# Adaptive-norm FFN with Strassen products on one core: two loads of SyncE's queue put in front of the first fetch of conditioning weights

## The chip, the cores and the metric

One core of a Trainium2 chip. The metric is the device time of one execution in microseconds (us); lower is better. The kernel before has 432.35 us as the median of 3 runs.

## The reference, cut to what matters

```python
W = L0_cond_weights[itok_B_0_15]                  # (64, 64, 64) picked out of 16 matrices
y = einsum('bct,bcd->bdt', x, W)                  # x: (64, 64, 1024), fp32
top1 = argmax(y_flat @ gate_w.T + expert_bias)    # 4 experts
base = einsum('bth,oh->bto', y, W_up)             # W_up: 1024 x 1024
delta = (y_flat @ lora_A[top1].T) @ lora_B[top1].T  # rank 8
out = x + base + delta
```

## The kernel before, in words

The 64 batch entries are taken in pairs (128 rows: two entries of 64 channels), and two pairs make a block, so there are 16 blocks of 256 rows. The product with W_up (1024 x 1024) is done for each block by a Strassen-like scheme of seven products of half size, named a11, a12, a22, s1, s2, s4 and s3. Each operand is split in a high and a low part, and a product is three matmuls per slice of 128. For that the rows of W_up must be transposed on TensorE (`turn_weights`, L632; L662), some of them after a sum or difference of quarters (`subtract`, L264: kinds 1 to 4, each for a row group c from 0 to 3), and every transposed group of 128x512 is then rounded by ScalarE (`split_turned`, L477; L493) and its low part made by VectorE (L893). There are 31 such groups in a written-out order, `TURNS` (L217), and PSUM banks are passed from one to another: a group waits until VectorE has finished the one that had its bank.

W_up arrives as eight pieces of 512 KB (`load_w_up`, L313), w_raw[0] to w_raw[7]; here they are called W0 to W7. The x of a pair is 512 KB too, x0 to x3 for the first two blocks. The first two blocks do not wait for the whole conditioning table. For each of their four pairs SyncE loads two indices into registers and fetches just the two 16 KB matrices that are needed (`load_first_cond`, L303; L309) into the tile y_small, which GpSimd has zeroed. TensorE needs both fetches and the x of the pair for `make_first_y` (L623, matmuls at L627), and ScalarE copies the result out (`move_first_y`, L439; L441). In later blocks `make_y` uses the whole table.

All these loads are issued on SyncE's queue in this order: W6, W7, W3, lora_B, W4, fetch 0 (two DMAs of 16 KB), x0, W2, W0, W5, W1, fetch 1, x1, x2, half of the table, x3, the other half, fetch 2, fetch 3. ScalarE issues the index, router and bias loads at the start.

TensorE's order in the start-up is written out at L735 to L815: warm-up transposes between the first groups (L738), then s4 of W4, two groups of lora_B, two warm-up transposes (L754), `make_first_y(0, 0)` (L756), s2 of W3, a11 of W2 (L758), `make_first_y(0, 1)`, s1 of W6, a12 of W2, a11 of W0 and so on; the first products (L679) follow. Block 1 onwards is a steady loop. In the start-up GpSimd does most of the `subtract` steps (L384 to L397), VectorE three of them (L1024, L1036, L1059) and the first `add_s1` (L1046, printed as L286), whose two inputs lie in SBUF.

Of the kernel before, what the change touches and what calls it, by code (L numbers as in the profile page):

```python
# [5 lines left out]
def adaln_ffn_kernel(  # L6
# [34 lines left out]

    B, C, T = x.shape
    S, _, D = cond_weights.shape
    O, _ = w_up.shape
    E, R, _ = lora_a.shape
# [24 lines left out]
    with ctx:  # L70
# [116 lines left out]
        def in_blocks(eng, period):  # L187
            with eng.Fori(0, BLOCKS // 2 - 1) as group:
                for n in range(2):
                    period(group * 2 + (n + 1), (n + 1) % 2, False)  # L190
            period(BLOCKS - 1, (BLOCKS - 1) % 2, True)

        def is_last(q):
            return isinstance(q, int) and q == BLOCKS - 1
# [4 lines left out]
        def x_part(par, t, half):  # L199
            return x_sb[:, 2 * par + t, half * BANK:(half + 1) * BANK]  # L200
# [9 lines left out]
        def first_cond(t):  # L210
            return y_small[:, t * P:(t + 1) * P]
# [10 lines left out]
                 ("a22", 3, p1)]  # L222
        GROUPS = [(op, c) for op, c, _ in TURNS]
        BANK_OF = [bank for _, _, bank in TURNS]
        FREED_BY = []
        for g in range(len(GROUPS)):
            same = [f for f in range(g) if BANK_OF[f] == BANK_OF[g]]
            FREED_BY.append(same[-1] + 1 if same else 0)
        LAST_OF = {op: 1 + max(g for g, (o, _) in enumerate(GROUPS) if o == op) for op, _ in GROUPS}
        AT = {name: g for g, name in enumerate(GROUPS)}  # L230

# [69 lines left out]
        @block.sync  # L301
        def _(sp):
            def load_first_cond(t):  # L303
                sp.wait_ge(index_loaded, 16)
                sp.wait_ge(first_zero, 1)
                for b in range(2):
                    rows = slice(b * C, (b + 1) * C)
                    index = sp.value_load(index_sb[0:1, 2 * t + b:2 * t + b + 1], min_val=0, max_val=S - 1)
                    sp.dma_start(first_cond(t)[rows, b * D:(b + 1) * D],  # L309
                                 cond_weights[bass.ds(index, 1), :, :].rearrange("s c d -> (s c) d"))\  # L310
                       .then_inc(first_loaded[t], 16)

            def load_w_up(c):  # L313
                sp.dma_start(w_raw[:, c, :], w_up[c * P:(c + 1) * P, :]).then_inc(w_up_loaded[c], 16)

            load_w_up(6)
            load_w_up(7)
            load_w_up(3)
            sp.dma_start(lora_b_sb[:, :, :, :], lora_b.rearrange("e (p j) r -> p e j r", p=P)).then_inc(lora_b_loaded, 16)
            load_w_up(4)  # L320
            load_first_cond(0)
            sp.dma_start(x_sb[:, 0, :], x_pairs[0]).then_inc(x_loaded[0], 16)
            load_w_up(2)
            load_w_up(0)
            load_w_up(5)
            load_w_up(1)
            load_first_cond(1)
            sp.dma_start(x_sb[:, 1, :], x_pairs[1]).then_inc(x_loaded[1], 16)
            sp.dma_start(x_sb[:, 2, :], x_pairs[2]).then_inc(x_loaded[2], 16)
            sp.dma_start(cond_sb[0:C, :, :], cond_rows).then_inc(cond_loaded[0], 16)  # L330
            sp.dma_start(x_sb[:, 3, :], x_pairs[3]).then_inc(x_loaded[3], 16)
            sp.dma_start(cond_sb[C:2 * C, :, :], cond_rows).then_inc(cond_loaded[1], 16)
            load_first_cond(2)
            load_first_cond(3)

            def store(q, par, t, half):
                sp.dma_start(out_pairs[2 * q + t, :, half * BANK:(half + 1) * BANK], x_part(par, t, half))\
                    .then_inc(stored[t], 16)

            def store_quarter(q, par, n):  # L340
                cols = slice(n * QUARTER, (n + 1) * QUARTER)
                sp.dma_start(out_pairs[2 * q + 1, :, cols], x_sb[:, 2 * par + 1, cols]).then_inc(stored[1], 16)

            def period(q, par, closing):
                sp.wait_ge(c11_out, q + 1)
                store(q, par, 0, 0)
                sp.wait_ge(c12_out, q + 1)
                store(q, par, 0, 1)
                if is_last(q):
                    sp.wait_ge(c21_out, q + 1)  # L350
                    store_quarter(q, par, 0)
                    sp.wait_ge(c22_out, q + 1)
                    store(q, par, 1, 1)
                    sp.wait_ge(last_out, 1)
                    store_quarter(q, par, 1)
                else:
                    sp.wait_ge(c21_out, q + 1)
                    store(q, par, 1, 0)
                    sp.wait_ge(c22_out, q + 1)
                    store(q, par, 1, 1)  # L360

            period(0, 0, False)
            in_blocks(sp, period)
            for t in range(2):
                sp.wait_ge(stored[t], 32 * BLOCKS + 16 * t)
# [802 lines left out]
```

## Time and profile before

| | |
|---|---|
| median of 3 runs | 432.35 us (431.86 to 432.89) |
| the profiled execution | 432.26 us, of which the span is 430.4 us |
| TensorE busy | 424.5 us (99% of the span) |
| VectorE busy | 358.3 us (83%) |
| ScalarE busy | 190.9 us (44%) |
| GpSimd busy | 117.4 us (27%) |
| granted TensorE clock | 1.000, mean |
| DMA | 38.85 MB, mean 90 GB/s |

PE is TensorE, ACT ScalarE, DVE VectorE, POOL GpSimd and SP SyncE; a q behind the name is the engine's queue. A row of the timeline gives the start in us from the start of the span, the duration, engine and line, then tile written and tiles read, and how many instructions were merged. Successive instructions of an engine overlap by some tenths of a microsecond. "us to landing" counts from an issue's start to the last of its data.

### The profile page before, as it was taken

What the parts mean: (1) busy time and instruction counts of PE and PEld (TensorE: products, weight loads), DVE (VectorE), ACT (ScalarE), POOL (GpSimd) and SP (SyncE); (2) the same over time, 40 slices, a digit from 0 to 9 for tenths busy, and PEclk for the clock granted to TensorE, in tenths of its full rate; (3) what the DMA queues carried; (4) which work ended last, traced back from release to release, by engine and by line L of the source; (5) the groups of instructions that cost most, each with busy time, mean ns of one, the idle gap of its engine ahead of it and who ended that gap; (6) DMA issues with size and microseconds to landing.
All of it is one profiled execution on the core that took longest, in us unless ns stands there. A gap on an engine that the chain in (4) does not pass through costs nothing.

```text
span 430.4 us, 8609 instructions
## 1 busy us (share of the span) xinstructions
PE 424.5 (99%) x2937; PEld 396.8 (92%) x2938; DVE 358.3 (83%) x648; ACT 190.9 (44%) x301; POOL 117.4 (27%) x92
## 2 busy tenths in 40 slices
PE   7999999999999999999999999999999999999997
PEld 7989999999999999999999999999999999999996
DVE  2998489797979979797997979799797989979773
ACT  3973463363625336262543626254263625426220
POOL 4971140503205050220505023050502305050230
DMA  7930140502214041230403123050312304031202
GB/s 266 353 55 3 50 149 24 170 18 86 96 44 151 24 130 42 86 107 34 161 24 123 47 79 116 24 171 24 122 49 64 131 24 171 24 122 49 80 19 97
DMA packets 18582, 38.85 MB, mean 90 GB/s; under 512 B 5094, under 2 KB 5350, under 8 KB 18570
## 3 DMA queue, kind: packets, MB, share of 16 engines
q1 hardware_dynamic: 14336, 23.86, 15.7%
q10 hardware_dynamic: 4234, 14.83, 11.4%
q8 instruction: 7, 0.11, 0.1%
q14 instruction: 5, 0.04, 0.0%
HBM read 21.91 MB, written 16.78 MB: 90 GB/s over the span
## 4 chain that ended last, share of the span: by engine, by line
PE 95%; ACT 3%; DVE 1%; issue 0%; POOL 0%; DVEq 0%; POOLq 0%; ACTq 0%
PE bank_x L679 23%; PE bank_y L679 23%; PE bank_c L679 20%; PE y_ps L619 11%; PE bank_b L679 10%; PE bank_x L738 1%; PE bank_y L685 1%; PE bank_x L685 1%; PE bank_c L685 1%; PE bank_b L685 1%; ACT w_s L493 1%; PE y_ps L627 1%; ACT w_a L493 1%; PE bank_y L716 1%; DVE w_s L893 0%; PE bank_c L694 0%
## 5 line engine op out<-in xcount | busy, mean ns | idle before, releaser
L286 POOL TENSOR_TENSOR s_sum<-a 128x512 f32<-128x512 f32 x15 | 19.5, 1301 | 283.4 <-DVE a L867 264.9
L432 ACT ACTIVATE x_hl<-x_sb 64x1024 fp32r<-64x1024 f32 x56 | 59.1, 1055 | 34.5 <-DMA out_dram<-x_sb 29.9
L862 DVE TENSOR_TENSOR x_hl<-x_sb,x_hl 64x1024 fp32r<-64x1024 f32 x56 | 68.3, 1220 | 1.7
L436 ACT ACTIVATE y_small<-y_ps 128x512 f32<-128x512 f32 x56 | 33.5, 597 | 57.7 <-PE y_ps L619 57.7
L619 PE MATMUL y_ps<-cond_hl,x_hl 128*128 x448 | 58.1, 273 | 0.0
L619 PEld LDWEIGHTS y_ps<-cond_hl,x_hl 128*128 128x128 f32 x448 | 54.7, 191 | 1.5 <-issue 0.2
L679 PE MATMUL bank_x<-w_a,hl_a 128*128 128x256 f32 (+1 forms) x408 | 54.1, 288 | 0.0
L679 PEld LDWEIGHTS bank_x<-w_a,hl_a 128*128 128x128 f32 x408 | 52.7, 188 | 0.4
L867 DVE TENSOR_TENSOR a<-y_ps,y_small 128x512 f32<-128x512 f32 x56 | 38.5, 687 | 16.7 <-ACT y_small L436 16.7
L679 PE MATMUL bank_y<-w_s,hl_s 128*128 128x292 f32 (+1 forms) x384 | 51.6, 290 | 0.0
L679 PE MATMUL bank_x<-w_s,hl_s 128*128 128x292 f32 (+1 forms) x384 | 51.5, 290 | 0.0
L679 PE MATMUL bank_y<-w_a,hl_a 128*128 128x292 f32 (+1 forms) x384 | 51.1, 289 | 0.0
L679 PEld LDWEIGHTS bank_y<-w_s,hl_s 128*128 128x128 f32 x384 | 49.8, 188 | 0.8 <-issue 0.2
L679 PEld LDWEIGHTS bank_x<-w_s,hl_s 128*128 128x128 f32 x384 | 49.8, 188 | 0.6
L679 PEld LDWEIGHTS bank_y<-w_a,hl_a 128*128 128x128 f32 x384 | 49.7, 188 | 0.2
L679 PE MATMUL bank_c<-w_s,hl_s 128*128 128x512 f32 x192 | 48.2, 399 | 0.0
L679 PE MATMUL bank_b<-w_s,hl_s 128*128 128x512 f32 x192 | 48.1, 399 | 0.0
L446 ACT ACTIVATE hl_a<-a 128x512 fp32r<-128x512 f32 x48 | 30.5, 636 | 36.1 <-DVE a L867 33.6
L679 PEld LDWEIGHTS bank_c<-w_s,hl_s 128*128 128x128 f32 x192 | 34.9, 188 | 7.3
L679 PEld LDWEIGHTS bank_b<-w_s,hl_s 128*128 128x128 f32 x192 | 35.2, 190 | 6.7
L679 PE MATMUL bank_c<-w_a,hl_a 128*128 128x512 f32 x168 | 41.2, 394 | 0.0
L872 DVE TENSOR_TENSOR hl_s<-s_sum,hl_s 128x512 fp32r<-128x512 f32 x32 | 37.2, 1170 | 3.5 <-ACT hl_s L446 2.0
(119 smaller groups left out, 566.8 us busy)
## 6 DMA issues: line engine op xcount, KB each, us to landing
out_dram<-x_sb SPq DMA_DIRECT2D x63, 256.0 KB, 2.0
x_sb<-in_x_dram ACTq DMA_DIRECT2D x28, 512.0 KB, 3.7
w_raw<-in_L_ffn_W_up_dram SPq DMA_DIRECT2D x8, 512.0 KB, 7.4
x_sb<-in_x_dram SPq DMA_DIRECT2D x4, 512.0 KB, 8.4
cond_sb<-in_L_cond_weights_dram SPq DMA_DIRECT2D x2, 256.0 KB, 9.6
out_dram<-x_sb SPq DMA_DIRECT2D x2, 128.0 KB, 1.9
router_sb<-in_L_ffn_lora_A_dram ACTq DMA_DIRECT2D x1, 128.0 KB
lora_b_sb<-in_L_ffn_lora_B_dram SPq DMA_DIRECT2D x1, 128.0 KB, 7.8
```

The source lines that it names most:

```text
L286: eng.tensor_tensor(s1_sum[:, :], a21[:, :], a22[:, :], ALU.add).then_inc(s1_added, 1)
L432: act.activation(x_hl[rows, t, b, :], x_sb[rows, 2 * par + t, :], ACT.Copy).then_inc(x_high, 1)
L436: act.activation(y_small[:, :].rearrange("q (g d) -> q g d", d=D), halves_of(y_ps)[:, :, 1, :], ACT.Copy).then_inc(y_small_out, 1)
L446: act.activation(hl[op][:, 0, :, :], src[:, :].rearrange("q (k n) -> q k n", n=P), ACT.Copy)\
L493: act.activation(turn_target(op, c, 0), bank.rearrange("q (k n) -> q k n", n=P), ACT.Copy)\
L619: mm = pe.matmul(y_ps[:, k % KH // 2, at:at + P], x_hl[:, t, b, k * P:(k + 1) * P], cond_hl[:, index[b], :, :], start=True, stop=True)
L627: mm = pe.matmul(FIRST_Y[2 * t + h][:, k * P:(k + 1) * P], x_sb[:, t, (h * KH + k) * P:(h * KH + k + 1) * P], first_cond(t), start=True, s ...
L679: mm = pe.matmul(dst, hl[op][:, a, k, :], w[:, b, k, cols], start=(fresh and k == 0 and a + b == 0), stop=(k == KH - 1 and a == 1), skip_g ...
L685: return pe.matmul(dst, z_t[t][:, :], src, start=False, stop=True, skip_group_check=True)
L862: dve.tensor_tensor(x_hl[other, t, b, :], x_sb[rows, 2 * par + t, :], x_hl[rows, t, b, :].bitcast(fp32), ALU.subtract).then_inc(x_low, 1)
L867: dve.tensor_tensor(dst[:, :].rearrange("q (g d) -> q g d", d=D), halves_of(y_ps)[:, :, 0, :], y_small[:, :].rearrange("q (g d) -> q g d", ...
L872: dve.tensor_tensor(hl[op][:, 1, :, :], src[:, :].rearrange("q (k n) -> q k n", n=P), hl[op][:, 0, :, :].bitcast(fp32), ALU.subtract).then ...
```

## The change

Of the two loads behind fetch 0, x0 and W2, both are now issued in front of it. Everything else keeps its place.

```diff
@@ -318,9 +318,9 @@
             load_w_up(3)
             sp.dma_start(lora_b_sb[:, :, :, :], lora_b.rearrange("e (p j) r -> p e j r", p=P)).then_inc(lora_b_loaded, 16)
             load_w_up(4)
-            load_first_cond(0)
             sp.dma_start(x_sb[:, 0, :], x_pairs[0]).then_inc(x_loaded[0], 16)
             load_w_up(2)
+            load_first_cond(0)
             load_w_up(0)
             load_w_up(5)
             load_w_up(1)
```

## Rows read from the trace of the kernel before

**Rows 1.** The page: shares of the chain that ended last, by engine.

```profile
PE 95%; ACT 3%; DVE 1%; issue 0%; POOL 0%; DVEq 0%; POOLq 0%; ACTq 0%
```

**Rows 2.** The chain that ended last, 0 to 55 us: start, us, what.

```profile
12.01 0.60 ACT w_s L493
...
22.38 0.50 ACT a L441
...
28.38 0.18 DVE partial L967
...
31.55 0.61 DVE w_raw L282
...
32.92 3.03 PE bank_x L679 x24
```

**Rows 3.** Timeline of SyncE's queue, 2.6 to 9.4 us.

```profile
2.65 0.69 SPq L314 DMA_DIRECT2D w_raw<-in_L_ffn_W_up_dram  x1
4.42 1.85 SPq L309 DMA_DIRECT2D y_small<-in_L_cond_weights_dram  x2
6.32 0.59 SPq L322 DMA_DIRECT2D x_sb<-in_x_dram  x1
6.95 2.38 SPq L314 DMA_DIRECT2D w_raw<-in_L_ffn_W_up_dram  x4
```

**Rows 4.** DMA issues: W4, fetch 0's second, x0, W2, fetch 3's last.

```profile
w_raw<-in_L_ffn_W_up_dram SPq DMA_DIRECT2D x1, 512.0 KB, 8.6
...
y_small<-in_L_cond_weights_dram SPq DMA_DIRECT2D x1, 16.0 KB, 5.8
...
x_sb<-in_x_dram SPq DMA_DIRECT2D x1, 512.0 KB, 6.3
...
w_raw<-in_L_ffn_W_up_dram SPq DMA_DIRECT2D x1, 512.0 KB, 7.0
...
y_small<-in_L_cond_weights_dram SPq DMA_DIRECT2D x1, 16.0 KB, 2.2
```

**Rows 5.** Windows: length, busy PE, PEld, DVE, ACT, POOL, granted clock, DMA share, GB/s.

```profile
12.00:13.00 1.00, 1.00 (x11) 1.00 (x10) 1.00 (x3) 0.99 (x2) 1.00 (x2) 1.00 1.06 430
...
17.00:32.00 15.00, 14.83 (x117) 13.78 (x115) 15.00 (x25) 12.33 (x24) 12.68 (x9) 1.00 0.58 124
```

**Rows 6.** Timeline of TensorE, 1.5 to 17 us.

```profile
1.53 3.46 PE L738 MATMUL bank_x<-ident 128*128 128x128 f32 x15 [1.53 <-POOL ident L371]
...
8.61 0.68 PE L640 MATMUL bank_c<-ident,router_sb 36*128 36x36 f32 x8 [1.20 <-DVE w_s L893]
...
12.90 1.06 PE L627 MATMUL y_ps<-y_small,x_sb 128*128 128x128 f32 x8
...
14.66 1.06 PE L627 MATMUL bank_y<-y_small,x_sb 128*128 128x128 f32 x8
...
15.99 1.04 PE L662 MATMUL y_ps<-ident,w_raw 128*128 128x128 f32 x8
```

**Rows 7.** Timeline of ScalarE, around 15.8 us.

```profile
15.84 0.62 ACT L441 ACTIVATE a<-bank_y 128x512 f32<-128x512 f32 x1
```

**Rows 8.** Timeline of VectorE, 17 to 25.5 us.

```profile
17.04 0.68 DVE L893 TENSOR_TENSOR w_s<-bank_c,w_s 128x512 fp32r<-128x512 f32 x1
17.63 0.72 DVE L270 TENSOR_TENSOR w_raw<-w_raw 128x512 f32<-128x512 f32 x1
...
21.86 0.68 DVE L872 TENSOR_TENSOR hl_a<-a,hl_a 128x512 fp32r<-128x512 f32 x1
...
23.66 1.80 DVE L286 TENSOR_TENSOR s_sum<-a 128x512 f32<-128x512 f32 x1
```

**Rows 9.** Timeline of GpSimd, 17.7 to 26.7 us.

```profile
17.76 1.75 POOL L278 TENSOR_TENSOR w_raw<-w_raw 128x512 f32<-128x512 f32 x1
...
23.63 1.28 POOL L282 TENSOR_TENSOR w_raw<-w_raw 128x512 f32<-128x512 f32 x1
...
24.87 1.75 POOL L282 TENSOR_TENSOR w_raw<-w_raw 128x512 f32<-128x512 f32 x1
```

## The prediction, made before the changed kernel ran

> **What bounds the kernel now.** I read the page first, for what the end hangs on. TensorE makes 95% of the chain that ended last [rows 1]; from 32.92 us on the chain is TensorE's products one behind another [rows 2]. So whatever shift the start-up has at 32.9 us arrives whole at the end, and the question is what sets that moment. The chain says it: ScalarE from 12.01 to 22.88 us without a gap, then TensorE, VectorE from 28.38 until its subtract ends at 32.16, then TensorE again [rows 2]. From 17 to 32 us VectorE is busy for all of the 15 us and TensorE for 14.83 [rows 5]. Three engines are nearly full there, and the chain changes between them.
>
> Next I read the loads, since the change touches only their order. SyncE finishes issuing W4 at 3.34 us, spends 1.08 us on the index registers, issues the two fetches from 4.42 to 6.27, x0 from 6.32, W2 from 6.95 [rows 3]. With the landing times of [rows 4], W4 lands at 2.65 + 8.6 = 11.25; the second fetch, issued in the last half of its row at about 5.8, at 5.8 + 5.8 = 11.6; x0 at 6.32 + 6.3 = 12.6; W2 at 6.95 + 7.0 = 13.95. They land in the order of issue, about 1.3 us apart for 512 KB, although a fetch of 16 KB would be small work; and the engines move 430 GB/s at 12 to 13 us, with a DMA share above 1 [rows 5]. I read this as one backlog served in order: SyncE issues some 6 us ahead of what lands.
>
> Last, the consumer. TensorE's first product with x0 has its first matmul at 12.90 [rows 6], right behind x0's landing at 12.6; the fetch was there 1.3 us before it. So x0 has no slack and the fetch has 1.3.
>
> **The change, part by part.**
>
> *SyncE.* x0 and W2 are issued from about 3.4 to 4.5 us (0.59 and some 0.5 us). Index loads and the fetches (1.08 + 1.85) follow and end near 7.4. W0 is issued within 0.1 us of where it was; W5, W1, fetch 1 and the rest don't move. No wait is added; the index wait is merely later. Cost on the issuing side: nothing.
>
> *The landings.* x0 and W2 have no longer the two fetches in front of them; these took what W4 to x0 (1.35 us) has over an ordinary 1.3, about 0.1. So x0 lands near 12.5 and W2 near 13.85. Gain: none on TensorE, since its warm-up transposes run until about 12.8 anyway. The fetch now lands behind W2 as it landed behind W4, 11.6 - 11.25 = 0.35 later: 13.85 + 0.3 = 14.1, at most 13.95 + 0.35 = 14.3. From the other side, if a fetch took its 5.8 us from issue whatever stands before it, its second half, now issued near 7.0, lands at 12.8. I take 14.1, because the rows show spacing by bytes in order, not a fixed delay: the last fetch of 16 KB, issued when the backlog was gone, took 2.2 us and not 5.8 [rows 4].
>
> The Trainium skill, DMA: Bandwidth & Descriptors, section "Anatomy of one DMA", puts a transfer at about 2.0 us plus its bytes at 436 GB/s (for GpSimd's path). By it a 16 KB fetch issued at 7.0 would land near 9.1, as an estimate from that page, before x0, and the change would cost nothing. The 2.2 us of the late fetch agrees with the page, the 5.8 us in the loaded stretch does not.
>
> *TensorE.* A first matmul follows a landing it waited for by some 0.15 us (I take this between 0 and the 0.3 by which 12.90 lies behind x0), so it starts at 14.26 instead of 12.90: 1.36 us later. All that stands behind it in TensorE's order moves too: s2 of W3, a11 of W2, the second half of y0 (matmuls from 14.66, end 15.72 [rows 6]), s1 of W6, the pair of groups at 15.99. W2 is not late for any of them.
>
> *ScalarE.* It copied the second half of y0 at 15.84 [rows 7], 0.12 us after TensorE ended it. Now that ends at 15.72 + 1.36 = 17.08 and the copy starts at 17.12: 1.28 us later. ScalarE is contiguous from there to 22.88 [rows 2], so it regains nothing by itself.
>
> *VectorE.* The low part at 17.04 [rows 8] becomes one at about 18.28 (TensorE, then ScalarE in front of it): 1.24 later. Behind it stands its own subtract, L270, at 17.63, now at 18.87. Here the order of two engines matters. The rows show that VectorE and GpSimd stand in each other's way when both read two SBUF operands: GpSimd's 1.28 us step took 1.75 beside L270 [rows 8, 9]; VectorE's L286, started at 23.66 just behind GpSimd's of 23.63, took 1.80 instead of 0.7 and ended 0.55 after GpSimd's end at 24.91; and GpSimd's next, from 24.87, ended 1.16 after VectorE's 25.46. Whoever is first finishes first. GpSimd's step of 17.76 (L278, W0) needs a11 of W0 transposed, which ends at 15.99 + 1.04 = 17.03, now 18.39. So it starts at 18.43, in front of VectorE's L270, and ends at 19.72; L270 ends at 19.72 + 0.55 = 20.27 instead of 18.35. Shift on VectorE: 1.92.
>
> From there each walks at its own pace. GpSimd waits for L270, then has three steps of 1.25 (W1, W0, W1): 20.31, 21.56, 22.79 to 24.08. VectorE's a11 operand (at 21.86 [rows 8]) comes at 21.86 + 1.92 = 23.78, is held to 24.63 (0.17 more) and holds GpSimd's fourth step to 24.63 + 1.16 = 25.79. VectorE reaches L286 at 23.66 + 1.92 + 0.17 = 25.75, and GpSimd its last L282 step at 25.75. It is a tie. If VectorE is first, L286 ends at 25.75 + 0.72 = 26.47, against 25.46 before: shift 1.0, since the wait of 1.1 us that it had is gone. If GpSimd is first, L286 ends at 25.75 + 1.28 + 0.55 = 27.6: shift 2.1.
>
> VectorE is contiguous from L286 to 32 us [rows 5]; at 28.38 it takes TensorE's first product, which, 1.4 to 1.6 us later, is still done before VectorE comes to it at 29.4. So the chain carries VectorE's shift: 1.0 in the first case, 2.1 in the second. TensorE, which waits for VectorE once more before 32.9, arrives there with 1.0 to 1.1, or 2.1.
>
> **The sum.** 1.36 on TensorE, 1.24 on VectorE, + 0.68 (L270 held) + 0.17 (operand held) - 1.1 (L286 not held) = 1.0, and 0.1 for TensorE's own lateness: **+1.1 us**. The profiled execution took 432.26 us, span 430.4; the sum gives 433.35. It lies 0.1 under the median of the runs, so on the median I forecast 432.35 + 1.1 = 433.45, put at **433.5**.
>
> **A rule on the two engines.** The Trainium skill, SBUF — State Buffer, says that VectorE and GpSimd share one pair of SBUF ports under an exclusive lock: the one that starts first keeps it for its whole instruction and the other is blocked, for a VectorE instruction with two SBUF inputs too. The 1.80 us of L286 agrees. Without this rule every shift would be the plain 1.24 to 1.36, and the sum +1.3.
>
> **The rivals.**
>
> *GpSimd wins the tie at L286*: all as above, +2.1, so 434.45. For it: before, GpSimd was ahead by 0.03 us there; against: two starts worked out to a tenth decide nothing. From 0.05 us on it decides whole.
>
> *The small fetch isn't behind W2*: it lands at 12.8 or earlier, TensorE starts within 0.1 us of before, and the time is 432.35 to 432.5. This is the case in which the change doesn't do what its order suggests. For it: the fetch is small, 32 KB in all. Against: it landed behind W4 before, and x0 behind it [rows 4]. The absorbed shift (waits that I think full turn out slack) comes to the same side: 432.4 to 433.0.
>
> *Faster*: one mechanism, the 1.1 us that VectorE's L286 spends behind GpSimd [rows 8]. If the fetch lands in time or nearly so, and the small shifts (x0 and W2 earlier by 0.1) put VectorE's L286 in front of GpSimd's step, at a TensorE delay under 0.5 us, the net is -0.2 to -1.1: 431.3 to 432.1. It decides from 0.03 us of order at 23.6; against it stand the landings.
>
> *The clock*: TensorE idles 1.3 us in front of y0. Before, it idled 1.20 us in front of 8.61 [rows 6], the granted clock is 1.00 in these windows [rows 5] and 1.000 as the mean of the span, and the transposes afterwards ran at 0.11 us each. If it fell to the lower of its two levels (1.2 of 2.4 GHz): the first 15 transposes took 3.46 us, 0.23 each, twice that pace; a stretch like it costs 3.46 / 2 = 1.7 more, in all 435.2. The Trainium skill, TensorE: Matmul & The Clock Gate, Part 1, has idleness close the gate again; the 1.20 us gap did not.
>
> **How the numbers follow.** Chances: the forecast 0.42; GpSimd first 0.27; fetch in time or shift absorbed 0.20; faster 0.06; clock 0.03; 0.02 for what I don't see. The range reaches from the fetch in time to GpSimd first with the landing at its late bound (+0.2 and something for noise): 432.2 to 434.8. A measurement of this kernel can tell about 0.2% (0.86 us) from no change. The forecast lies close above that at +1.1, so I give a fifth of it to "same", and with the rivals: slower 0.65, same 0.28, faster 0.07.
>
> **What would show it.** On SyncE's queue, x0 at 3.4 and the fetches at about 5.5 to 7.3. The fetch landing 7 us after its issue, x0 some 9 us after its own. TensorE idle about 1.3 us before its first L627 matmul, at 14.2 and released by that load; ScalarE's copy at 15.84 now near 17.1. VectorE's L270 at 1.4 us instead of 0.72, and L286 at 0.7 (forecast) or 1.8 (first rival). The first product of the second row of the chain (32.92) at 33.9 to 35. If TensorE's first L627 starts before 13.1, the backlog reading is wrong; if it starts at 14.2 and the end is not later by a microsecond, the chain through ScalarE and VectorE was not as full as I read it.

## The result, and the profile after

The changed kernel takes 435.36 us (435.12 to 435.42, 4 runs) against 432.36 us: 3.0 us more, ratio 1.0061 with a 95% interval of 1.0035 to 1.0087 (ratios here and below are the recorded ones; the two medians alone give 1.0069). A second set of 10 runs gave 435.38 us, ratio 1.0059 (1.0043 to 1.0076). It is slower, as forecast, but by 3.0 us and not 1.1, outside the range (432.2 to 434.8). The profiled execution took 435.42 us, its span 433.6.

The chain that ended last, 0 to 60 us of the kernel after (start, us, what):

```profile
6.77 7.84 DMA y_small<-in_L_cond_weights_dram
14.61 0.14 issue
14.75 1.13 PE y_ps L627 x8
...
19.50 1.43 DVE w_raw L270
...
24.52 0.86 DVE hl_a L872
...
26.63 3.30 PE bank_x L679 x24
...
34.53 0.61 DVE w_raw L282
...
35.91 3.04 PE bank_x L679 x24
```

Before, no DMA stood in this stretch of the chain, and ScalarE's groups filled it up to 22.88 us [rows 2]. Now it starts with the second half of the small fetch, which takes 7.84 us to land, and then TensorE, a short piece of ScalarE, and VectorE from 18.80 to 26.59 us. TensorE's first product (26.63) waits for VectorE's last low part there, and from 30.76 us on the chain is VectorE's again. L286 and the steps next to it run beside that product and are not in the chain as the profile draws it; VectorE is nevertheless busy without a gap from 19.50 us on, so its delays add up in its own timeline, below. The product that was at 32.92 in [rows 2] is at 35.91: +2.99, the whole difference.

SyncE's queue of the kernel after, from 2.6 to 9.8 us (SPq is SyncE's queue):

```profile
2.65 0.63 SPq L314 DMA_DIRECT2D w_raw<-in_L_ffn_W_up_dram  x1
3.33 0.50 SPq L321 DMA_DIRECT2D x_sb<-in_x_dram  x1
3.87 0.45 SPq L314 DMA_DIRECT2D w_raw<-in_L_ffn_W_up_dram  x1
5.39 1.95 SPq L309 DMA_DIRECT2D y_small<-in_L_cond_weights_dram  x2
7.38 2.43 SPq L314 DMA_DIRECT2D w_raw<-in_L_ffn_W_up_dram  x3
```

DMA issues of the kernel after, one by one: W4, x0, W2, the fetch's second half (KB, us to landing):

```profile
w_raw<-in_L_ffn_W_up_dram SPq DMA_DIRECT2D x1, 512.0 KB, 8.9
...
x_sb<-in_x_dram SPq DMA_DIRECT2D x1, 512.0 KB, 9.5
...
w_raw<-in_L_ffn_W_up_dram SPq DMA_DIRECT2D x1, 512.0 KB, 10.4
...
y_small<-in_L_cond_weights_dram SPq DMA_DIRECT2D x1, 16.0 KB, 7.8
```

W4 lands at 11.55, x0 at 12.8, W2 at 14.3, the fetch at 14.6, in the order of issue. x0 is issued 3.0 us earlier than before and lands 0.2 us later. TensorE, the timeline of the kernel after:

```profile
14.75 1.13 PE L627 MATMUL y_ps<-y_small,x_sb 128*128 128x128 f32 x8 [1.36 <-DMA y_small<-in_L_cond_weights_dram]
```

It starts 1.85 us behind its 12.90 of [rows 6], and TensorE was idle for 1.36 us in front of it. Then ScalarE, VectorE and GpSimd, the timelines of the kernel after, with the rows that answer to [rows 7 to 9]:

```profile
17.68 0.60 ACT L441 ACTIVATE a<-bank_y 128x512 f32<-128x512 f32 x1 [0.19 <-PE bank_y L627]
```

```profile
18.80 0.69 DVE L893 TENSOR_TENSOR w_s<-bank_c,w_s 128x512 fp32r<-128x512 f32 x1 [0.48 <-ACT w_s L493]
19.50 1.43 DVE L270 TENSOR_TENSOR w_raw<-w_raw 128x512 f32<-128x512 f32 x1
...
24.44 0.94 DVE L872 TENSOR_TENSOR hl_a<-a,hl_a 128x512 fp32r<-128x512 f32 x1
...
26.50 1.81 DVE L286 TENSOR_TENSOR s_sum<-a 128x512 f32<-128x512 f32 x1
...
29.43 0.81 DVE L872 TENSOR_TENSOR hl_s<-s_sum,hl_s 128x512 fp32r<-128x512 f32 x1
```

```profile
19.10 1.28 POOL L278 TENSOR_TENSOR w_raw<-w_raw 128x512 f32<-128x512 f32 x1 [0.86 <-PE y_ps L662]
...
24.78 1.73 POOL L282 TENSOR_TENSOR w_raw<-w_raw 128x512 f32<-128x512 f32 x1
...
26.48 1.28 POOL L282 TENSOR_TENSOR w_raw<-w_raw 128x512 f32<-128x512 f32 x1
```

In GpSimd's rows L278 is `subtract` of kind 2 and L282 of kind 4. Read VectorE's starts against [rows 8]: +1.76 at 18.80, +1.87 at L270. L270 is 0.71 longer, because GpSimd's L278 had begun at 19.10 and ran until 20.38; before, L270 was first by 0.13 us. L872 is 0.26 longer (GpSimd's third step of kind 2 was running). L286 is as long as before, 1.81, and starts 2.84 late: GpSimd's last L282 was 0.02 us in front of it. L872 at 29.43 is 0.13 longer. That makes 1.87 + 0.71 + 0.26 + 0.13 = 2.97.

TensorE's first product started here in the kernel before:

```profile
24.21 3.27 PE L679 MATMUL bank_x<-w_a,hl_a 128*128 128x292 f32 x24
```

Now it starts at 26.63 and ends at 29.93, 2.4 us late, because VectorE's low part in front of it ends at 26.59. So TensorE itself was 2.4 us late by then, and VectorE 3.0.

### The profile page after: what moved, and what is told of

Its sections match the earlier page's. It is cut to its first block, busy times and chain, and to the rows that moved or that the text cites. A ratio compares the mean times of both kernels' runs of the same rounds, so it can differ in the third digit from the quotient of the medians.

```text
span 433.6 us, 8609 instructions
## 1 busy us (share of the span) xinstructions
PE 426.1 (98%) x2937; PEld 396.8 (91%) x2938; DVE 360.4 (83%) x648; ACT 191.3 (44%) x301; POOL 116.6 (27%) x92
## 4 chain that ended last, share of the span: by engine, by line
PE 93%; DVE 3%; DMA 2%; SPq 1%; issue 0%; ACT 0%; DVEq 0%
PE bank_x L679 23%; PE bank_y L679 23%; PE bank_c L679 19%; PE y_ps L619 11%; PE bank_b L679 10%; DMA y_small<-in_L_cond_weights_dram 2%; PE y_ps L627 1%; DVE w_s L893 1%; PE bank_x L685 1%; PE bank_y L685 1%; PE bank_c L685 1%; PE bank_b L685 1%; DVE w_a L893 1%; PE bank_y L716 1%; SPq L314 1%; PE bank_c L694 0%
## 5 line engine op out<-in xcount | busy, mean ns | idle before, releaser
L286 POOL TENSOR_TENSOR s_sum<-a 128x512 f32<-128x512 f32 x15 | 19.5, 1301 | 283.5 <-DVE a L867 265.0
L872 DVE TENSOR_TENSOR hl_s<-s_sum,hl_s 128x512 fp32r<-128x512 f32 x32 | 38.1, 1197 | 2.7 <-ACT hl_s L446 1.0
```

Of the source, the lines that this page charges most:

```text
L286: eng.tensor_tensor(s1_sum[:, :], a21[:, :], a22[:, :], ALU.add).then_inc(s1_added, 1)
L872: dve.tensor_tensor(hl[op][:, 1, :, :], src[:, :].rearrange("q (k n) -> q k n", n=P), hl[op][:, 0, :, :].bitcast(fp32), ALU.subtract).then ...
```

## The experiments

Twelve kernels ran. The first two are the pair again, unchanged. Where nothing else is said, the lines are an edit of the changed kernel. Ratios are against the kernel before, run beside each set.

**e1_before.** No edit.

> The kernel before, unchanged, to see how much the load stream moves from one profiled execution to the next. In the two traces at hand W4 lands at 11.27 us before and 11.59 after the change, and the loads behind it are 0.34 to 0.5 us later too, although nothing in front of W4 was moved. Theory A (that lateness varies from execution to execution): W4 lands anywhere from 11.2 to 11.6 here, W2 2.7 us behind it, and the time is 431.9 to 432.9. Theory B (the two earlier issues slow the stream themselves): W4 lands at 11.25 to 11.3 here.

Measured: 432.47 us, ratio 1.000 (0.9983 to 1.0017), W4 8.7 us from issue to landing against 8.6 in [rows 4].

**e2_after.** No edit.

> The kernel after, unchanged, as the pair of the run above. Both theories: fetch 0 lands 0.3 us behind W2, TensorE's first product with x0 starts 0.15 us behind that, and the time is near 435.4. Theory A: W4 lands between 11.2 and 11.6; where it is early, the first product starts at 14.4 instead of 14.75. Theory B: W4 lands at 11.55 to 11.65 again.

Measured: 435.38 us; W4 8.9 us again, first product at 14.86. Theory A falls: here and below, the four profiles with the order of before have W4 at 8.6, 8.7, 8.7 and 8.6 us from its issue (always at 2.65 to 2.70), the nine that issue something else right behind W4 have 8.8 to 9.3. The loads from W4 on are late with the new order, W4 itself included.

**e3_x0_only.** Shown against the kernel before.

```diff
-            load_first_cond(0)
             sp.dma_start(x_sb[:, 0, :], x_pairs[0]).then_inc(x_loaded[0], 16)
+            load_first_cond(0)
             load_w_up(2)
```

> Only x0 in front of fetch 0; W2 stays behind it. The theory of a backlog served in order: the fetch lands 0.3 us behind x0, near 12.9 to 13.2, and TensorE's first product with x0 starts 0.2 to 0.5 us later than before. If shifts are carried plainly, the time is 432.6 to 432.9. If the port order between VectorE and GpSimd adds to them: VectorE's L270, which was 0.13 us ahead of GpSimd's L278, falls behind it, takes 1.2 to 1.9 us instead of 0.72, and the time is 433.4 to 434.0. The rival that a small fetch overtakes 512 KB loads: no difference to before.

Measured: 434.35 us, ratio 1.0035 (1.0017 to 1.0053), single runs from 432.96 to 435.15. Its profiled execution is one of 434.55 us. TensorE, VectorE and GpSimd in it:

```profile
13.76 1.02 PE L627 MATMUL y_ps<-y_small,x_sb 128*128 128x128 f32 x7
...
18.51 1.73 DVE L270 TENSOR_TENSOR w_raw<-w_raw 128x512 f32<-128x512 f32 x1
...
18.41 1.28 POOL L278 TENSOR_TENSOR w_raw<-w_raw 128x512 f32<-128x512 f32 x1
```

The product is 0.86 late, more than I expected. In this execution two things end together in front of it: the fetch lands at 13.65 (issued at 6.35, 7.3 us to landing), and W4, 9.3 us from its issue, landed at 11.9 and TensorE worked from then on without a gap until 13.70. So this run alone doesn't show that the fetch held the product. L270 costs another 1.01, since GpSimd was ahead by 0.10 us. 0.9 us of lateness became 2.3 at the product that was at 32.92. Two of the ten runs, at 433.0 and 433.2, may have had the other order of the two engines; they were not profiled.

**e4_three.**

```diff
             load_w_up(2)
-            load_first_cond(0)
             load_w_up(0)
+            load_first_cond(0)
```

> x0, W2 and W0 in front of fetch 0: one load of 512 KB more than in the changed kernel. Backlog in order: the fetch lands 1.3 us later than in the changed kernel (15.5 to 15.9), TensorE's first product with x0 starts at 15.7 to 16.1, 2.9 to 3.2 later than before. The end is that plus what VectorE waits for GpSimd (0 to 1.8 us): 435.3 to 437.2, and more than the changed kernel's by about 1.3 less or plus one collision. The rival that the fetch takes a fixed time from its issue: 0.5 us later than in the changed kernel, 435.9.

Measured: 438.19 us, ratio 1.0121 (1.008 to 1.0163): later than either theory said. The first product starts at 15.96, +3.06, as the backlog reading has it: the fetch's second half, issued at 7.31, took 8.5 us and landed at 15.8. (The row below names VectorE's L891 as what ended the wait. In the changed kernel the product began before that instruction had ended, so it doesn't wait for it.) What I had not reckoned with is the clock. TensorE's timeline, then windows (length, busy PE, PEld, DVE, ACT, POOL, granted clock, DMA share, GB/s) of this kernel:

```profile
15.96 1.93 PE L627 MATMUL y_ps<-y_small,x_sb 128*128 128x128 f32 x8 [2.71 <-DVE lora_b_hl L891]
17.68 1.06 PE L662 MATMUL bank_b<-ident,w_raw 128*128 128x128 f32 x4
```

```profile
14.00:16.00 2.00, 0.04 (x1) 0.07 (x1) 1.91 (x2) 0.72 (x1) 1.88 (x3) 1.00 1.01 390
16.00:18.00 2.00, 2.00 (x10) 2.00 (x11) 0.00 (x0) 0.07 (x1) 0.77 (x1) 0.52 1.05 377
18.00:20.00 2.00, 2.00 (x13) 2.00 (x12) 0.59 (x1) 1.49 (x3) 0.25 (x1) 0.62 1.10 327
20.00:22.00 2.00, 2.00 (x21) 2.00 (x20) 1.13 (x3) 1.69 (x4) 1.06 (x2) 1.00 1.19 176
```

After 2.71 us of idle the granted clock is at its lower level (0.52 and 0.62 as means of two windows, 1.2 GHz for most of them), and four transposes take 1.06 us instead of 0.60. After the 1.36 us of the changed kernel it stayed at 1.00. VectorE was 3.6 us late at the first low part behind y0, 4.7 at L270, and 5.85 behind its last meeting with GpSimd.

**e5_w2_only.** Shown against the kernel before.

```diff
-            load_first_cond(0)
-            sp.dma_start(x_sb[:, 0, :], x_pairs[0]).then_inc(x_loaded[0], 16)
             load_w_up(2)
+            load_first_cond(0)
+            sp.dma_start(x_sb[:, 0, :], x_pairs[0]).then_inc(x_loaded[0], 16)
```

> Only W2 in front of fetch 0; x0 stays behind it. Backlog in order: the fetch lands 0.3 us behind W2 at the place that x0 had (12.9 to 13.6), and x0 at the place that W2 had (13.95 to 14.6). The first product with x0 now waits for x0 and starts at 14.1 to 14.8. If the lateness of the first product is all that counts, and not which input is late, the time is near that of the changed kernel, 434.8 to 435.5. The rival that something is special about the fetch itself (its register loads, its small packets): 432.4 to 433.5, since the fetch is only one load later.

Measured: 435.04 us, ratio 1.0056 (1.0042 to 1.007). TensorE in this kernel:

```profile
14.54 1.13 PE L627 MATMUL y_ps<-y_small,x_sb 128*128 128x128 f32 x8 [1.07 <-DMA x_sb<-in_x_dram]
```

Now x0 is the late one, landing at 14.4, and the time is nearly the same. So it isn't something special about the fetch: the last input of the first product counts, and with it that input's rank in the queue.

**e6_fetch_act.** The queue of the changed kernel, with the fetch on ScalarE's.

```diff
             load_w_up(2)
-            load_first_cond(0)
             load_w_up(0)
...
+            load_first_cond_act(0)
```

The added line stands on ScalarE, behind the bias load.

> The order of the changed kernel on SyncE's queue, but fetch 0 is issued on ScalarE's queue behind the bias load, so it stands behind no 512 KB load in its ring. Backlog theory: the fetch lands by 6 to 9 us; the first product waits for x0 alone and starts at 12.7 to 13.2; L270 is in front of GpSimd's L278 again; the time is that of the kernel before or a little under, 432.0 to 432.7. The rival that x0 and W2 being issued earlier costs by itself (a stream that is 0.3 us later): first product at 13.0 to 13.2, L270 behind L278 as in the run with x0 alone, 433.4 to 434.5.

Measured: 432.87 us, ratio 1.0015 (0.9998 to 1.0033). The ten runs fall in two groups, six from 432.56 to 432.94 and four from 433.96 to 434.21; the profiled execution is one of 432.65, and what follows holds for it. The second group, inside the rival's range, was not profiled. The faster group is near the time of before, but by another way than I expected. DMA issues of this kernel, the fetch's second half:

```profile
y_small<-in_L_cond_weights_dram ACTq DMA_DIRECT2D x1, 16.0 KB, 8.2
```

Issued by ScalarE at 4.77 us, it still lands near 13.0 and not at 6 to 9, so another queue did not let it pass here. Whether the bias load in front of it held it or the loads of SyncE's queue is not separated by any run. It is no later than x0 (13.2), and the first product starts at 13.32, +0.42, behind TensorE's own work, which runs without a gap from W4's landing at 11.7. VectorE and GpSimd:

```profile
24.05 0.69 DVE L286 TENSOR_TENSOR s_sum<-a 128x512 f32<-128x512 f32 x1
...
26.16 1.54 DVE L883 TENSOR_TENSOR hl_s<-s_sum,hl_s 128x512 fp32r<-128x512 f32 x1 [0.22 <-ACT hl_s L457]
...
24.03 1.86 POOL L282 TENSOR_TENSOR w_raw<-w_raw 128x512 f32<-128x512 f32 x1
```

Here VectorE won the tie at L286, which took 0.69 instead of 1.80, though GpSimd's step is again recorded 0.02 us in front. It was 0.73 us ahead of before with the next low parts, lost 0.31 waiting for ScalarE, then met GpSimd's next step at 26.16, was held for 0.86, and left 0.44 late, about what it had come with. **In this execution the whole gain of the won tie was gone one meeting later.** e7 and e11 show that this is no rule: there half of the gain or more stayed.

**e7_after_pool.**

```diff
             subtract(pool, 2, 1)
+            add_s1(pool, 0)
...
-            add_s1(dve, 0)
```

> The changed kernel with the first add_s1 (L286, 1.81 us on VectorE, of which some 1.1 behind GpSimd) given to GpSimd, behind its subtract of kind 2 for group 1. Theory that VectorE's chain from 19.5 us on carries the loss and that L286 is part of it: VectorE is 1.7 us ahead behind the place of L286, until it waits for TensorE's first product near 30 us; the time falls by 0.9 to 1.5, to 433.9 to 434.5. The rival that TensorE's own lateness of 1.85 us carries it: no fall over 0.3.

Measured: 434.59 us, ratio 1.0046 (1.0032 to 1.006): 0.8 under the changed kernel, just short of the 0.9 to 1.5 expected. VectorE no longer has L286, 1.7 us of its chain, but its next operand step was then held by GpSimd:

```profile
28.03 1.73 DVE L873 TENSOR_TENSOR hl_s<-s_sum,hl_s 128x512 fp32r<-128x512 f32 x1
```

**e8_before_pool.** The same edit on the kernel before.

> The kernel before with the same change: the first add_s1 on GpSimd. VectorE was the chain from 28.38 to 32.16 us there, and TensorE had 0.4 to 0.8 us of idle in that stretch. By the same theory the time falls by 0.4 to 0.8, to 431.6 to 432.0. The rival: no change, since GpSimd's subtracts of kind 4 and add_s2 come later by what VectorE gains.

Measured: 431.86 us (431.68 to 432.15, 10 runs), ratio 0.9983 (0.9969 to 0.9997). It is faster than both kernels, by 0.4 us against before, and bears out that VectorE's chain was a bound there.

**e9_l270_later.**

```diff
-            subtract(dve, 3, 1)
             split_turned("a12", 2)
+            subtract(dve, 3, 1)
```

> The changed kernel with VectorE's subtract L270 behind one more low part (a12 of W2), so that it starts when GpSimd's L278 (19.1 to 20.4 us) has ended. Theory of a lock between VectorE and GpSimd: L270 takes 0.68 to 0.85 us instead of 1.43, and what is gained (0.3 to 0.4 us) may be given back at the next meeting, VectorE's L872 of operand a11, which now comes earlier in GpSimd's last step of kind 2 and is held for up to 0.6 us longer; time 435.0 to 435.4. The rival that L270 is long because of its operands or its waits: 1.4 us wherever it stands.

Measured: 435.5 us, ratio 1.0068 (1.0046 to 1.009). VectorE in this kernel:

```profile
20.45 0.68 DVE L270 TENSOR_TENSOR w_raw<-w_raw 128x512 f32<-128x512 f32 x1
...
24.04 1.54 DVE L872 TENSOR_TENSOR hl_a<-a,hl_a 128x512 fp32r<-128x512 f32 x1
```

The same instruction on the same operands takes 0.68 us once GpSimd's step (19.14 to 20.42) is over. So 0.75 of the 1.43 was waiting. And L872, now 0.4 us earlier, waited 0.6 longer: nothing gained.

**e10_indices_first.** The four index registers' loads of SyncE in front of x0; the order of the DMAs unchanged.

```diff
+            index = first_indices(0)
             sp.dma_start(x_sb[:, 0, :], x_pairs[0]).then_inc(x_loaded[0], 16)
             load_w_up(2)
-            load_first_cond(0)
+            fetch_first_cond(0, index)
```

> The changed kernel with SyncE's register loads of both indices done before x0 is issued; the order of all DMAs is that of the changed kernel, but x0 is issued about 1 us or more later, near 4.5 to 5 us. Theory C (issuing x0 and W2 while lora_B's 512 small packets are still being served slows these, and so all behind them): lora_B lands at 9.9 to 10.05 instead of 10.32, W4 at 11.25 to 11.4, the fetch at 14.2 to 14.4, the first product starts near 14.45, time 434.9 to 435.2. Rival D (it is the fetch's absence between W4 and x0, or chance): W4 at 11.5 to 11.7 still, 435.3 to 435.5.

Measured: 435.18 us, ratio 1.0061 (1.0039 to 1.0083). x0 is issued at 4.75 instead of 3.33, W4 lands 8.7 us after its issue, as in the order of before, but the fetch at 14.5, above the 14.2 to 14.4 of theory C, and the product at 14.64. It supports theory C in W4's landing, and only in part in what follows: x0 and W2 land 0.2 us earlier than in the changed kernel, the fetch 0.1. It is one profile, and why an issue behind it slows a load in front of it is left open.

**e11_after_l270_pool.**

```diff
+            subtract(pool, 3, 1)
             subtract(pool, 1, 1)
...
-            subtract(dve, 3, 1)
```

> The changed kernel with the subtract L270 given from VectorE to GpSimd, in front of its subtract of kind 1 for group 1. VectorE loses an instruction of 1.43 us from its chain at 19.5 us and meets no GpSimd step there; GpSimd is 0.3 us later from there on (it had waited for L270 until 21.07). Theory that VectorE's chain carries the loss: VectorE is 1.4 us ahead at first; what it meets later (L872, L286) may take up to 0.9 back; time 433.9 to 434.9. Rival: no change.

Measured: 434.44 us, ratio 1.0043 (1.003 to 1.0056), 0.9 under the changed kernel, as expected. The profiled execution is one of 434.92, with loads 0.3 us later. In it VectorE met GpSimd at operand a11 (23.68 us, 1.44 long) and at L286 (26.24, 1.82).

**e12_before_l270_pool.** The same edit on the kernel before.

> The kernel before with the subtract L270 given to GpSimd. VectorE loses 0.72 us from a full chain, GpSimd gets 1.28 more and loses 0.46 of waiting. By the theory of VectorE's chain the time falls by 0 to 0.6 (431.8 to 432.4), unless GpSimd's later steps of kind 4 and add_s2 become what VectorE waits for (then up to 433).

Measured: 433.26 us, ratio 1.0026 (1.0011 to 1.0041): 0.9 slower, where I had expected a gain and at most 433. Of VectorE's 0.72 us less, 0.27 was left at L286, the rest having gone mostly into a wait for ScalarE at 17.99, and one later meeting cost 1.07:

```profile
26.40 1.75 DVE L873 TENSOR_TENSOR hl_s<-s_sum,hl_s 128x512 fp32r<-128x512 f32 x1
```

## Why the prediction was right or wrong

**Right: where the loss comes from.** The backlog served in order (e4 and e5 move the late input by one load each, as it asks; e3 agrees but doesn't decide), the fetch 0.3 us behind W2, no gain from x0's earlier issue, the idle TensorE in front of y0, ScalarE passing it on, L270 caught behind L278 (0.68 forecast, 0.71 measured), operand a11 held (0.17 forecast, 0.26 measured), and the whole shift carried from 32.9 us to the end. "The small fetch isn't behind W2" fell.

**Wrong, first: the step "The landings".** I let the loads behind W4 come 0.1 us earlier than before, and they came 0.2 to 0.3 later, 0.3 to 0.5 behind the forecast: the fetch at 14.6, not 14.1. I took what stands in front of a moved load as untouched by it; the profiles show W4 itself late by 0.3 (8.9 against 8.6, again in e2_after). TensorE's shift was 1.85, not 1.36, VectorE's 1.87 at L270 where I had 1.24. That is 0.6 of the missing 1.9 us.

**Wrong, second, and the larger: the term -1.1 for L286.** I worked out both engines at 25.75, a tie, and took VectorE as first, with a gain of 1.1, without a row that says so. L286 took 1.81, the gain was 0, and this is the first rival. The rows of before spoke for GpSimd: there too one of its steps lay beside the a11 operand and waited for it [rows 8, 9], and GpSimd came out 0.03 us ahead at L286. In all twelve profiles that have L286 on VectorE, GpSimd's step is recorded 0.01 to 0.03 us in front; in eleven VectorE lost (1.80 to 1.82), in e6 it won (0.69). So starts this close don't tell who wins; what does is not found.

The prize was put too high as well. The product that I had 1.4 to 1.6 us late was 2.4 late, and before, TensorE had 0.2 us of idle between it and 32.92 (at 32.30). By these rows the end would have been some 2.2 us late even with the tie won, so that the tie was worth about 0.8. This is an estimate; no run tests it, though e7, without L286 on VectorE, lies at 0.8. A further meeting, L872 at 29.43 (0.13), was not in my sum. Term by term, forecast and measured: 1.24 and 1.87, 0.68 and 0.71, 0.17 and 0.26, -1.1 and 0, 0 and 0.13, and 0.1 and 0 for TensorE's own lateness.

The rival with GpSimd first gave 434.45, 0.9 under the measured value: 0.6 from the first error, the rest from the held steps. With both ends (the late landing bound of 14.3, and the lost tie) my range still stopped at 434.8; it had no allowance for loads in front of the moved ones getting slower.

**The lock.** The Trainium skill, SBUF — State Buffer, section "SBUF: two separate sides", says that whichever of VectorE and GpSimd starts first on their shared ports keeps them for its whole instruction. The runs agree: L270 1.43 behind GpSimd, 0.68 alone (e9), 1.73 when GpSimd had started 0.10 us before it (e3). In e6 the engine recorded first by 0.02 us was the one held, so the order of two recorded starts isn't exact to that.

**The other rule.** The Trainium skill, DMA: Bandwidth & Descriptors, section "Anatomy of one DMA", gives about 2.0 us plus the bytes at 436 GB/s for a transfer on GpSimd's path; by it, as an estimate, the fetch would have landed some 2 us after its issue. The trace disagrees in the loaded stretch. The same 16 KB took 5.8 us from issue with the order of before, 7.8 with two more loads in front of it, and 8.5 with three (e4).

**The clock.** It stayed at 1.00 after 1.36 us of idle; that rival fell for this change, but in e4 it is real, after 2.71 us. From y0's first matmul to the start of its second half TensorE took 1.84 us in the changed kernel (14.75 to 16.59) and 3.43 in e4 (15.96 to 19.39): 1.6 more, near the 1.7 at which I had priced it. In e4 the Trainium skill, TensorE: Matmul & The Clock Gate, Part 1, which has idleness close the gate, is borne out.

## What to carry to other kernels

In a loaded stretch a DMA's place in the queue counted far more than its size or its issue time (16 KB landed 7.8 us after issue; x0, issued 3.0 us earlier, landed 0.2 later): put the small load that a consumer needs in front of the big ones, and find the last input of each consumer before moving anything. When a start-up is packed so that several engines take turns as the bound, a delay is not merely carried; it changes who is first on a shared resource, and 1.85 us became 3.0. To shorten such a stretch, take an instruction off the engine that is full (e8: 0.4 us), and look at every later meeting before counting the gain (e12: 0.9 us lost by the same kind of move). Before counting on a shorter chain, look how late the next engine already is: it takes over as the bound.

## What the runs showed that I had not expected

A load already issued landed later when others were issued right behind it: W4 at 8.8 to 9.3 us from its issue in nine profiles, 8.6 or 8.7 in four with the fetch behind it, and 8.7 where x0 was issued 1.4 us later (e10). What does this inside the queue was not found.

A 16 KB fetch on ScalarE's queue, its second half issued at 4.77 us, landed at about the same time as the 512 KB of x0 issued on SyncE's at 3.31 (13.0 against 13.2 us): here a second queue was no express lane.

Behind 2.71 us of idle TensorE the granted clock was down for some 3 us of start-up work, at about twice the time per transpose (four in 1.06 us instead of 0.60); behind 1.36 and 1.45 us (the changed kernel, twice) it was not.
